# An attention and feed-forward kernel on one core: where V is made, when the Gram products run, and how the last two steps are ordered

## Chip, cores and metric

One core of a Trainium2 chip. The metric is the device time of one execution in microseconds. The kernel before took 211.31 us, the median of three runs (209.78 to 213.27).

## What is computed

x has 8 sequences of 1024 rows of 128 channels, float32. Two layers follow each other, each with a residual and a layer norm.

```python
def _L0_attn_ref(...):                       # 16 heads of 8 channels
    def proj_heads(W, bb):
        z = x + x @ W.T + bb                 # and split into heads
    q, k1, k2, v1, v2 = ...                  # five of these
    S1 = einsum('bhnd,bhne->bhde', k1, v1) / n
    S2 = einsum('bhnd,bhne->bhde', k2, v2) / n
    v1m, v2m = v1.mean(over rows), v2.mean(over rows)
    S12 = S1 * S2
    out = q@S1*v2m*g1 + S12.sum(axis=2)*g2 + q@S2*v1m*g3 + q@S12*g4
    return layernorm(out) * ln_g + ln_b  @ Wo.T + bo
def _L0_ffn_ref(...):                        # only expert 0 counts
    x = tgt + relu(tgt @ w1[0] + b1[0]) @ w2[0] + b2[0]
    return layernorm(x) * gamma + beta
x = layernorm(x + attn(x)); x = layernorm(x + ffn(x))
```

Attention has no softmax, so for each sequence it is a 128x128 matrix. It follows from the Gram matrix G = xᵀx (with the column sums of x beside it). S1 and S2 are heads of (I+Wk) G (I+Wv)ᵀ with terms for the biases.

## The kernel before

The rows are tiled in 16 groups of 512 (4 tiles of 128), two groups to a sequence (a "batch" in the code). A program of steps n = -2 to 15 runs on each engine (`run_steps`, `body`). In step n TensorE does, in this order: the products of x with the sequence's matrix for group n+1 (`product`, 16 matmuls into `z_ps`), `up` of group n (four chunks of the feed-forward's first weights), the transposes of x of group n+2 (`turn_x`), `down` of group n (16 matmuls of 128x128), and the transposes of x1 of group n+1 (`turn_x1`). ScalarE squares, takes roots, does the relus and writes the results; VectorE adds, takes statistics (`stats`), normalizes, and splits x, x1 and the matrices in a high and a low part for fp32r; POOL (GpSimd) adds and multiplies rows out of SBUF. Each engine's list is in a fixed order written out by hand, and semaphores join them, so an instruction that waits holds all that stands behind it on its engine.

**Preparing a sequence.** `gram(b)` makes G of sequence b in 8 matmuls, `gram_out` copies it. `gram_av(b)` makes two products: G·A_v (256 columns, for E), and the column sums, broadcast to 128 weight columns, with A_v (256 columns: V, the same row on all partitions). VectorE turns them to E (L769) and V (L775) and signals both by one semaphore, EV_out. `ak_e(b)` on TensorE, which waits for it, makes A_k·E; `s_out` makes S1 and S2 of it and V; `prepare(b)` makes M (on POOL, from batch 1 on); `attention_matrix(b)` and `centered(b)` make the matrices P and Q; ScalarE and VectorE split them (`PQ_upper`, `PQ_rest`). Even steps n from 2 to 12 prepare sequence (n+2)/2. Sequences 0 to 4 have their Gram products in steps -2 and -1; those of 5, 6 and 7 stand at the ends of steps 7, 9 and 11, around `turn_x1`.

**The start (step -2).** bv1 and bv2 are spread from HBM to 128 partitions, 64 KB each, on ScalarE's queue, behind the small vectors. The "late" vectors (ln_g, ln_b, b1) go on POOL's queue behind Wo and Wq; `turn_late` on TensorE waits for them and stands ahead of `ak_e(0)`. SP's queue carries x of sequence 0, Wk1, Wk2 and x of the others. `output_rows` needs the late vectors and Wo.

**The end (steps 14, 15 and what follows).** The last group's `down` goes in two halves to two PSUM banks. Behind step 15 VectorE runs `half_y2`, `half_y2n`, `half_y3`, `half_st4` and `half_res`: residual, statistics, normalizing, gamma, beta, again statistics and normalizing, half by half; POOL does y3 of half 0. ScalarE takes the roots between (`half_std`) and writes the results of group 14 (`result`, L580). The y2g and y3 of group 14 are on VectorE (L824, L827).

Of the kernel before, what the change touches and what calls it, by code (L numbers as in the profile page):

```python
# [42 lines left out]
EARLY = 5  # L43


def build(nc, x, Wq, bq, Wk1, bk1, Wk2, bk2, Wv1, bv1, Wv2, bv2, g1, g2, g3, g4, ln_g, ln_b, Wo, bo,
# [11 lines left out]
    with ctx:  # L58
# [24 lines left out]
        g_row = sb("g_row", [1, 4, HEADS])  # L83
        scale_row = sb("scale_row", [1, 128])
# [21 lines left out]
        V_sb = sb("V_sb", [128, 2, 128])  # L106
        S_sb = sb("S_sb", [128, 2, 128])
# [57 lines left out]
        bv_loaded = sem("bv_loaded")  # L165
# [51 lines left out]
        EV_out = sem("EV_out")  # L217
# [24 lines left out]
        end_y2n = sem("end_y2n")  # L242
        end_y2g = [sem("end_y2g0"), sem("end_y2g1")]
        end_y3 = [sem("end_y30"), sem("end_y31")]
# [3 lines left out]
        end_res = sem("end_res")  # L248
# [58 lines left out]

        def rows(t, n=TILES):
            return t.unsqueeze(1).to_broadcast([128, n, 128])
# [4 lines left out]
        def half_y3(eng, h):  # L314

            two_tiles, own = slice(2 * h, 2 * h + 2), (GROUPS - 1) % 2
            eng.wait_ge(end_y2n, h + 1)
            eng.tensor_tensor(y2g[:, two_tiles, :], y2n[:, two_tiles, :], rows(gamma_rows[:, :], 2), ALU.mult).then_inc(end_y2g[h], 1)
            eng.wait_ge(end_y2g[h], 1)
            eng.wait_ge(x1beta_out, GROUPS)  # L320
            eng.tensor_tensor(y3[own][:, two_tiles, :], y2g[:, two_tiles, :], x1beta[own][:, two_tiles, :], ALU.add).then_inc(end_y3[h], 1)

        def s_out(dve, b):

            wait(dve, EV_out, b + 1)
            wait(dve, s_done, b + 1)
            for j in range(2):
                last = dve.scalar_tensor_tensor(out=S_sb[:, j, :], in0=V_sb[:, 1 - j, :],
                                                scalar=cols[:, j:j + 1],
                                                in1=prep_ps[:, j * 128:(j + 1) * 128],  # L330
                                                op0=ALU.mult, op1=ALU.add)
            last.then_inc(S_out, 1)

        def prepare(eng, b):

            eng.wait_ge(EV_out, b + 1)
# [3 lines left out]
            eng.tensor_tensor(gv[:, :, :], V_sb[:, :, :], gmask[:, 0:2, :], ALU.mult).then_inc(m_step, 1)  # L340
# [18 lines left out]
        class Step:  # L359
            def __init__(self, n):  # L360
# [12 lines left out]
                self.gram = n % 2 == 1 and has(3) and self.seq(3) >= EARLY  # L373
# [12 lines left out]
        VECTORS = 16 * (4 + 3)  # L386
# [7 lines left out]
        def _(sp):  # L394
# [6 lines left out]
            for i, w in enumerate((Wk1, Wk2)):  # L401
                sp.dma_start(w_raw[:, 2 + i, :], w[:, :]).then_inc(kv_loaded, 16)
            for b in range(1, BATCHES):
                load_x(b)

            def store(b):
                for g in range(1 if b == BATCHES - 1 else SEQ_GROUPS):
                    wait(sp, res_out, b * SEQ_GROUPS + (g + 1))
# [4 lines left out]
            for h in range(2):  # L413
                t = TILES + 2 * h
                sp.wait_ge(end_res, h + 1)
# [7 lines left out]
        def _(pool):  # L423
# [25 lines left out]
            for i, v in enumerate((ln_g, ln_b)):  # L449
                pool.dma_start(late_rows[i:i + 1, :], row(v)).then_inc(late_loaded, 16)  # L450
            pool.dma_start(late_rows[2:6, :], b1[0, :].rearrange("(k c) -> k c", c=128)).then_inc(late_loaded, 16)
# [21 lines left out]
            def body(st):  # L473
# [6 lines left out]
                if st.prev and not st.last:  # L480
# [7 lines left out]
                if st.prev2 and not st.prep:  # L488
                    result_bias(n - 2)
# [24 lines left out]
            half_y3(pool, 0)  # L514
# [3 lines left out]
        def _(act):  # L518
            for i, w in enumerate((Wv1, Wv2)):
                act.dma_start(w_raw[:, i, :], w[:, :]).then_inc(kv_loaded, 16)  # L520
            for i, v in enumerate((bk1, bk2, bq)):
                act.dma_start(vec_rows[i:i + 1, :], row(v)).then_inc(vec_loaded, 16)
            for i, g in enumerate((g1, g3, g4, g2)):
                act.dma_start(g_row[:, i, :], row(g)).then_inc(vec_loaded, 16)
            for i, v in enumerate((bv1, bv2)):
                act.dma_start(bv_rows[:, i, :], spread(v)).then_inc(bv_loaded, 16)
# [5 lines left out]
            def less_bv():  # L532
                act.wait_ge(bv_loaded, 16 * 2)
                act.activation(nbv_rows[:, 0, :], bv_rows[:, 1, :], ACT.Copy, scale=float(SEQ))
                act.activation(nbv_rows[:, 1, :], bv_rows[:, 0, :], ACT.Copy, scale=float(SEQ)).then_inc(nbv_ready, 1)
# [16 lines left out]
            def squares(m):  # L552
# [8 lines left out]
                std(z_sum[:, :], std1, std1_out, 1.0 / C)  # L561

# [36 lines left out]
            def body(st):  # L599
# [7 lines left out]
                if st.prev:  # L607

                    wait(act, st3_out, n)
                    std(two(st3, 2), std3, std3_out, 1.0 / C)  # L610
                if st.nxt:
                    squares(n + 1)
                if st.cur:
# [4 lines left out]
                    relu(st, 2)  # L618
                    relu(st, 3)
# [11 lines left out]
                if st.prev2:  # L631

                    wait(act, st4_out, n - 1)
                    std(two(st4, 2), std4, std4_out, 1.0 / C)
# [6 lines left out]
                if st.nxt:  # L641
# [8 lines left out]
                if st.gram:  # L650
                    gram_out(st.seq(3))
# [10 lines left out]
            act.wait_ge(st4_out, GROUPS - 1)  # L662
            std(two(st4, 2), std4, std4_out, 1.0 / C)
            half_std(st3, std3, 1, end_st3, end_std3)
# [467 lines left out]
```

## Time and profile before

| | |
|---|---|
| median of 3 runs | 211.31 us |
| profiled execution | 209.8 us, its span 208.1 us |
| granted TensorE clock, mean | 0.989 of 2.4 GHz |
| TensorE busy | 191.7 us (92%), 1377 instructions |
| VectorE busy | 161.8 us (78%), 478 |
| GpSimd (POOL) busy | 136.3 us (66%), 177 |
| ScalarE busy | 127.8 us (61%), 383 |
| chain that ended last | PE 73%, DVE 12%, issue 4%, DMA 4%, POOL 4%, ACT 2% |

The profile is one execution. PE is TensorE's matmuls (L904 is a helper through which all of them go, so they are told apart by their tiles), PEld its weight loads, DVE is VectorE, ACT ScalarE, SP the engine that issues most DMAs. A product of float32 operands is two records of the profile, one of fp32r operands is one. Busy shares are means over stages that have different limits; what holds a stage is read from the chain of waits and from the waits themselves.

### The profile page before, as it was taken

How to read it: one execution, taken by the hardware profiler on the slowest of the kernel's cores; microseconds unless marked ns; L12 is line 12 of the kernel's file. 1: busy time of each engine (PE TensorE's matmuls, PEld its weight loads, DVE VectorE, ACT ScalarE, POOL GpSimd, SP SyncE). 2: the span in 40 equal slices, each digit the busy share in tenths (PEclk: the TensorE clock that was granted, in tenths of full speed). 3: DMA queues.
4: the chain of work that ended last, by engine and by line, in shares of the span. 5: the costliest groups of instructions: out<-in, count | busy, mean ns of one | idle time of the engine just before them, and what ended most of it. 6: DMA issues, size and time to landing. Idle time of an engine off the chain costs nothing.

```text
span 208.1 us, 4250 instructions
## 1 busy us (share of the span) xinstructions
PE 191.7 (92%) x1377; PEld 176.2 (85%) x1377; DVE 161.8 (78%) x478; ACT 127.8 (61%) x383; POOL 136.3 (66%) x177
## 2 busy tenths in 40 slices
PE   6949999999999999999999999999999999999930
PEld 6838998998898979897989999998989899988620
DVE  0265854988879887989698787977798869896895
ACT  0342439364659575966596667758585659785571
POOL 8904651474697758984898379756897389876130
PEclk9999999999999999999999999999999999999995
DMA  5999700000000100110010101010011001011012
GB/s 154 243 191 289 185 0 5 2 0 5 0 15 35 54 2 0 55 50 0 0 54 4 48 3 50 2 54 0 2 50 55 0 3 50 0 52 54 2 50 101
DMA packets 12116, 9.98 MB, mean 48 GB/s; under 512 B 727, under 2 KB 9950, under 8 KB 12094
## 3 DMA queue, kind: packets, MB, share of 16 engines
q1 hardware_dynamic: 11056, 8.52, 13.2%
q0 software_dynamic: 448, 0.92, 2.5%
q10 hardware_dynamic: 590, 0.26, 0.6%
q8 instruction: 11, 0.18, 0.3%
q14 instruction: 11, 0.09, 0.1%
HBM read 5.51 MB, written 4.19 MB: 47 GB/s over the span
## 4 chain that ended last, share of the span: by engine, by line
PE 73%; DVE 12%; issue 4%; DMA 4%; POOL 4%; ACT 2%; DVEq 0%; POOLq 0%; ACTq 0%
PE down_ps L904 25%; PE up_ps L904 20%; PE prep_ps L904 11%; PE z_ps L904 10%; DMA late_rows<-in_L_ffn_b 4%; PE turn_ps L1031 3%; PE turn_ps L1002 2%; DVE y2n L705 2%; DVE st L700 2%; DVE down_ps L749 2%; DVE E_sb L769 1%; DVE x1T_lo L840 1%; DVE y2n L870 1%; DVE V_sb L775 1%; ACT res L580 1%
## 5 line engine op out<-in xcount | busy, mean ns | idle before, releaser
L904 PE MATMUL down_ps<-w_sb,hT 128*128 128x128 f32 x496 | 61.0, 277 | 0.1
L904 PEld LDWEIGHTS down_ps<-w_sb,hT 128*128 128x128 f32 x496 | 58.4, 192 | 1.2 <-DVE y2n L705 0.4
L597 ACT ACTIVATE hT<-up_ps,cols 128x512 f32<-128x512 f32 x64 | 41.7, 681 | 4.4 <-PE up_ps L904 4.2
L580 ACT ACTIVATE res<-y,nb,rstd 128x128 f32<-128x128 f32 x60 | 24.7, 483 | 7.5 <-POOL nb L471 7.5
L509 POOL TENSOR_TENSOR x1b<-x,b_rows 128x512 f32<-128x512 f32 x16 | 20.6, 1286 | 10.1 <-DVE x L705 10.1
L904 PE MATMUL up_ps<-x1T_hi,w_hi 128*128 128x512 f32 x64 | 26.0, 406 | 0.5 <-ACT hT L597 0.5
L904 PE MATMUL up_ps<-x1T_lo,w_hi 128*128 128x512 f32 x64 | 25.4, 398 | 0.0
L904 PE MATMUL up_ps<-x1T_hi,w_lo 128*128 128x512 f32 x64 | 25.3, 396 | 0.0
L558 ACT ACTIVATE z_sq<-z_ps 128x128 f32<-128x128 f32 x64 | 16.8, 270 | 11.4 <-PE z_ps L904 11.4
L498 POOL TENSOR_TENSOR xu<-X,u_rows 128x512 f32<-128x512 f32 x16 | 19.0, 1187 | 6.0 <-DVE u_rows L696 6.0
L705 DVE TENSOR_SCALAR x<-z_ps,st,rstd 128x128 f32<-128x128 f32 x64 | 21.9, 404 | 0.1
L483 POOL TENSOR_TENSOR y2g<-y2n,gamma_rows 128x512 f32<-128x512 f32 x14 | 18.0, 1284 | 5.8 <-DVE y2n L705 5.8
L705 DVE TENSOR_SCALAR y2n<-down_ps,st,rstd 128x128 f32<-128x128 f32 x60 | 20.5, 405 | 0.5
L511 POOL TENSOR_TENSOR x1beta<-x,beta_rows 128x512 f32<-128x512 f32 x16 | 20.6, 1291 | 0.0
L904 PE MATMUL z_ps<-PQ_hi,xT_hi 128*128 128x256 f32 x64 | 20.5, 321 | 0.0
L799 DVE SCALAR_TENSOR_TENSOR z_ps<-z_ps,rstd,xu 128x128 f32<-128x128 f32 x64 | 18.2, 353 | 0.6
L487 POOL TENSOR_TENSOR y<-y2g,x1beta 128x512 f32<-128x512 f32 x14 | 17.8, 1273 | 1.1
L550 ACT ACTIVATE std<-st,eps_col 128x4 f32<-128x4 f32 x46 | 12.3, 295 | 9.6 <-DVE st L700 9.6
L904 PE MATMUL z_ps<-PQ_hi,xT_lo 128*128 128x256 f32 x64 | 18.0, 281 | 0.0
L904 PE MATMUL z_ps<-PQ_lo,xT_hi 128*128 128x256 f32 x64 | 17.9, 280 | 0.0
L904 PE MATMUL z_ps<-PQ_hi,spread 128*128 128x256 f32 x64 | 17.9, 279 | 0.0
L340 POOL TENSOR_TENSOR gv<-V_sb,gmask 128x256 f32<-128x256 f32 x7 | 5.2, 746 | 17.2 <-DVE V_sb L775 17.2
(151 smaller groups left out, 416.5 us busy)
## 6 DMA issues: line engine op xcount, KB each, us to landing
X<-in_L_attn_x SPq DMA_DIRECT2D x8, 512.0 KB, 9.9
out<-res SPq DMA_DIRECT2D x15, 256.0 KB, 2.0
w_sb<-in_L_ffn_w POOLq DMA_DIRECT2D x2, 256.0 KB, 9.8
out<-res SPq DMA_DIRECT2D x2, 128.0 KB, 1.9
w_raw<-in_L_attn_Wv ACTq DMA_DIRECT2D x2, 64.0 KB, 2.8
w_raw<-in_L_attn_Wk SPq DMA_DIRECT2D x2, 64.0 KB, 4.0
bv_rows<-in_L_attn_bv ACTq DMA_DIRECT2D x2, 64.0 KB, 6.0
g_row<-in_L_attn_g ACTq DMA_DIRECT2D x4, 0.1 KB
```

The source lines that it names most:

```text
L483: pool.tensor_tensor(y2g[:, :, :], y2n[:, :, :], rows(gamma_rows[:, :]), ALU.mult).then_inc(y2g_out, 1)
L487: pool.tensor_tensor(y3[(s - 1) % 2][:, :, :], y2g[:, :, :], x1beta[(s - 1) % 2][:, :, :], ALU.add).then_inc(y3_out, 1)
L498: pool.tensor_tensor(xu[s % 2][:, :, :], X[:, b, g * TILES:(g + 1) * TILES, 0:C], rows(u_rows[:, :]), ALU.add).then_inc(xu_out, 1)
L509: pool.tensor_tensor(x1b2[(s + 1) % 2][:, :, :], x1[:, :, :], rows(b2_rows[:, :]), ALU.add).then_inc(x1b2_out, 1)
L511: pool.tensor_tensor(x1beta[(s + 1) % 2][:, :, :], x1[:, :, :], rows(beta_rows[:, :]), ALU.add).then_inc(x1beta_out, 1)
L550: act.activation(dst[:, :], src, ACT.Sqrt, bias=eps_col[:, :], scale=scale).then_inc(done, 1)
L558: act.activation(z_sq[:, t, :], z_ps[t // 2][:, t % 2 * 256:t % 2 * 256 + C], ACT.Square, accum_out=z_sum[:, t:t + 1]).then_inc(sq_out, 1)
L580: last = act.activation(res[buf][:, t, :], y3[buf][:, t, :], ACT.Identity, scale=rstd4[:, t:t + 1], bias=nb4[:, t:t + 1])
L597: act.activation(hT[:, k, :], up_ps[k % len(up_ps)][:, :], ACT.Relu, bias=cols[:, 5 + k:6 + k]).then_inc(relu_out, 1)
L705: last = dve.tensor_scalar(dst[:, t, :], of_tile(t), st[:, t // 2, 3 * (t % 2) + 1:3 * (t % 2) + 2], rstd[:, t:t + 1], ALU.subtract, ALU.mult)
L799: last = dve.scalar_tensor_tensor(out=y1_tile(t), in0=y1_tile(t), scalar=rstd1[:, t:t + 1], in1=xu[(s + 1) % 2][:, t, :], op0=ALU.mult, op ...
L904: return pe.matmul(o, lhsT, rhs, start=start, stop=stop)
```

## The change

1. For sequences 2 to 7 `gram_av` makes only G·A_v. Their V comes from two products (`v_rows`): the column sums of three sequences are the three weight columns, and the result is three rows of 256. VectorE adds bv (`v_rest`), and SP spreads each row to 128 partitions by a DMA (`place_v`). E and V have a semaphore each.
2. The Gram products of sequences 5, 6, 7 stand in steps 1, 3, 5.
3. bv is loaded as one row and spread by a product with ones; ScalarE copies and scales it. The late vectors are on SP's queue, ahead of x(1).
4. E, V and A_k·E of sequence 1 are made in step -2, ahead of P of sequence 0; its S behind `PQ_rest(0)`. `ak_e(1)` writes a bank of its own.
5. In step 14 VectorE takes the statistics of y3(12) behind those of y1(15), and those of y3(13) and its root in the same step; in step 15 ScalarE takes the root of y2(14) behind three relus. y2g and y3 of group 14 are on POOL.
6. The last group: y2d = (y2 − mean)·gamma and y3 = y2d·rstd + x1beta, each a fused instruction, half by half on VectorE. The result of half 0 is on ScalarE. The second half of `down` goes to z_ps[0], the first to prep_ps.

```diff
+VSET = 3
-        last_ps = [down_ps[:, 0:2 * C], prep_ps[:, 0:2 * C]]
+        last_ps = [prep_ps[:, 0:2 * C], z_ps[0][:, 0:2 * C]]
+        bv_ps = up_ps[0][:, 0:256]
+        def s_bank(b):
+            return up_ps[1] if b == 1 else prep_ps
+        def v_of(b):
+            return V_sb[:, :, :] if b < 2 else V_all[:, b - 2, :, :]
...
-                self.gram = n % 2 == 1 and has(3) and self.seq(3) >= EARLY
+                self.gram = EARLY + n // 2 if n in (1, 3, 5) else None
+                self.v_set = {0: 0, 7: 1}.get(n)
+                self.v_rest = {1: 0, 7: 1}.get(n)
...   SP
+            for i, v in enumerate((ln_g, ln_b)):
+                sp.dma_start(late_rows[i:i + 1, :], row(v)).then_inc(late_loaded, 16)
+            sp.dma_start(late_rows[2:6, :], b1[0, :].rearrange("(k c) -> k c", c=128)).then_inc(late_loaded, 16)
             for b in range(1, BATCHES):
                 load_x(b)
+            def place_v(v):
+                sp.wait_ge(rows_out, v + 1)
+                for i in range(VSET):
+                    sp.dma_start(V_all[:, v * VSET + i, :, :]..., V_rows[i:i + 1, v, :, :]...to_broadcast([1, 128, 256])).then_inc(V_landed[v], 16)
             def store(b):
                 for g in range(1 if b == BATCHES - 1 else SEQ_GROUPS):
+                    if (b, g) in ((0, 0), (2, 1)):
+                        place_v(b // 2)
...   POOL
+                if st.last:
+                    result_bias(n - 2)
-                if st.prev and not st.last:
+                if st.prev:
...   ScalarE
+            for i, v in enumerate((bv1, bv2)):
+                act.dma_start(bv_row[:, i, :], row(v)).then_inc(vec_loaded, 16)
             for i, g in enumerate((g1, g3, g4, g2)):
                 act.dma_start(g_row[:, i, :], row(g)).then_inc(vec_loaded, 16)
-            for i, v in enumerate((bv1, bv2)):
-                act.dma_start(bv_rows[:, i, :], spread(v)).then_inc(bv_loaded, 16)
             def less_bv():
-                act.wait_ge(bv_loaded, 16 * 2)
+                act.wait_ge(bv_done, 1)
+                act.activation(bv_rows[...], bv_ps, ACT.Copy).then_inc(bv_ready, 1)
...
+                    if st.last:
+                        root3(n)          # between relu 2 and relu 3
+                if st.nxt and not st.nxt2:
+                    root4(n - 1)          # behind x1T_hi
             half_std(st3, std3, 0, end_st3, end_std3)
-            act.wait_ge(st4_out, GROUPS - 1)
-            std(two(st4, 2), std4, std4_out, 1.0 / C)
             half_std(st3, std3, 1, end_st3, end_std3)
+            root4(GROUPS - 2)
+            half_std(st_end, std_end, 0, end_st4, end_std4)
             result(GROUPS - 2, GROUPS % 2, BATCHES - 1)
-            half_std(st4, std4, 0, end_st4, end_std4)
-            half_std(st4, std4, 1, end_st4, end_std4)
+            half_std(st_end, std_end, 1, end_st4, end_std4)
+            act.wait_ge(end_nb, 1)
+            for t in range(2):
+                last = act.activation(res[own][:, t, :], y3[own][:, t, :], ACT.Identity, scale=rstd_end[...], bias=nb_end[...])
...   VectorE, step -2
                     prepare(dve, 0)
                     u_row()
+                    e_and_v(1)
                     xT_rest(0)
                     PQ_rest(0)
+                    s_out(dve, 1)
...   VectorE, step 14
                     stats(y1_pairs, st2, st2_out)
+                if st.nxt and not st.nxt2:
+                    y3_stats(n - 2, s % 2)
...
                     normalize(x1, y1_tile, st2, rstd2, x1_out)
-                if st.last:
-                    ...                   # y2g and y3 of group 14
+                if st.nxt and not st.nxt2:
+                    y3_stats(n - 1, 1 - s % 2)
...
+                if st.nxt and not st.nxt2:
+                    result_factors(n - 1)
...   VectorE, the end
+            half_y2(0); half_y2d(0); half_y3(0)
+            half_y2(1); half_y2d(1)
+            y3_stats(GROUPS - 2, 1 - own)
+            half_st4(0)
+            half_y3(1)
+            result_factors(GROUPS - 2); result_bias_here(GROUPS - 2)
+            half_st4(1)
+            half_r4(0)
+            dve.scalar_tensor_tensor(out=nb_end[:, half[0]], ...).then_inc(end_nb, 1)
+            half_r4(1)
+            ...                           # res of half 1, two tensor_scalar
...   TensorE
                 pe.transpose(vec_ps[:, 0:3], vec_rows[:, :], ident[0:3, 0:3])
+                mm(bv_ps, ones[0:1, :], bv_row[...]).then_inc(bv_done, 1)
             def gram_av(b):
+                if b >= 2:
+                    wait(pe, G_out, min(BATCHES, b + 4))
+                    mm(prep_ps[:, 0:256], G_sb[:, b, 0:C], A_kv[:, 0:2, :]...).then_inc(ev_done, 1)
+                    return
+            def v_rows(v):
+                b = 2 + v * VSET
+                pe.wait_ge(G_out, b + VSET)
+                pe.wait_ge(PQfix_out, 2 if v == 0 else 5)
+                mm(prep_ps[0:VSET, 0:256], G_sb[:, b:b + VSET, C], A_kv[:, 1:3, :]...).then_inc(rows_done, 1)
...   TensorE, step -2
                     turn_late()
+                    keep_warm(2)
                     ak_e(0)
                     output_rows()
                     gram(1, range(SEQ_TILES))
+                    gram_av(1)
                     attention_matrix(0)
                     centered(0)
+                    ak_e(1)
...   TensorE, step -1
-                    gram_av(1)
+                    pe.wait_ge(nbv_ready, 1)
                     gram(2, range(0, 3))
-                    product(0, 0, lambda: ak_e(1))
+                    product(0, 0)
...   TensorE, steps 0 to 15
                     up(n, 0)
                 if st.prep:
                     ak_e(st.prepared())
+                if st.v_set == 1:
+                    v_rows(1)
...
+                if st.v_set == 0:
+                    v_rows(0)             # last of step 0
```

## Rows read from the trace of the kernel before

**Rows 1.** Stages: window, its length, busy us of each engine, granted clock, DMA

```profile
10.00:20.00 10.00, 6.70 (x49) 6.02 (x48) 5.25 (x17) 3.25 (x10) 2.83 (x3) 1.00 1.00 230
...
39.19:60.92 21.73, 21.22 (x154) 19.43 (x154) 18.14 (x54) 13.15 (x41) 14.88 (x18) 1.00 0.00 1
...
104.40:127.17 22.77, 22.77 (x171) 21.32 (x170) 18.97 (x57) 15.67 (x49) 16.64 (x21) 1.00 0.07 25
...
199.30:208.10 8.80, 0.00 (x0) 0.00 (x0) 6.07 (x20) 3.13 (x10) 1.72 (x2) 0.73 0.25 89
```

**Rows 2.** Waits of TensorE over the whole run: us, times, longest

```profile
PE z_ps L930 <- DMA late_rows<-in_L_ffn_b: 2.2, 1, 2.2
...
PE prep_ps L904 <- DVE V_sb L775: 1.5, 3, 0.5
```

**Rows 3.** The chain of waits in order of time: start, us, what

```profile
5.30 7.52 DMA late_rows<-in_L_ffn_b
...
15.03 1.79 PE up_ps L904 x16
16.82 0.35 PE prep_ps L904 x4
...
25.75 0.46 POOL M_sb L351
...
30.06 1.88 PE z_ps L904 x16
...
51.88 0.34 DVE V_sb L775
...
116.28 0.86 PE prep_ps L904 x4
...
118.79 0.44 PE prep_ps L904 x4
```

**Rows 4.** Timeline of the start: start us, us, engine, line, operation

```profile
1.59 4.26 PE L904 MATMUL down_ps<-ident 128*128 128x128 f32 x20 [1.59 <-POOL ident L428]
...
9.00 1.10 PE L904 MATMUL prep_ps<-A_kv,G_sb 128*128 128x256 f32 x4
...
11.93 0.48 DVE L769 SCALAR_TENSOR_TENSOR E_sb<-bv_rows,G_sb,prep_ps 128x256 f32<-128x256 f32 x1 [2.63 <-DMA bv_rows<-in_L_attn_bv]
...
14.35 0.46 PE L904 MATMUL z_ps<-WoT,lnb_wide 128*128 128x128 f32 x2 [0.63 <-ACT Wog L544]
```

**Rows 5.** DMAs: issuer, count, KB each, median us from issue to landing

```profile
out<-res SPq DMA_DIRECT2D x15, 256.0 KB, 2.0
...
w_raw<-in_L_attn_Wk SPq DMA_DIRECT2D x2, 64.0 KB, 4.0
bv_rows<-in_L_attn_bv ACTq DMA_DIRECT2D x2, 64.0 KB, 6.0
```

**Rows 6.** Timeline of VectorE in step 8, which a Gram product precedes

```profile
117.76 0.42 DVE L775 TENSOR_TENSOR V_sb<-prep_ps,nbv_rows 128x256 f32<-128x256 f32 x1
```

**Rows 7.** Timeline of the last two steps and the end

```profile
188.84 0.20 POOL L471 TENSOR_TENSOR nb<-mr,minus 128x4 f32<-128x4 f32 x1
...
193.37 0.30 ACT L550 ACTIVATE std<-st,eps_col 128x4 f32<-128x4 f32 x1 [2.16 <-DVE st L700]
193.57 2.47 ACT L597 ACTIVATE hT<-up_ps,cols 128x512 f32<-128x512 f32 x4
...
197.11 0.69 DVE L827 TENSOR_TENSOR y<-y2g,x1beta 128x512 f32<-128x512 f32 x1
...
197.21 0.65 POOL L471 TENSOR_TENSOR nb<-mr,minus 128x4 f32<-128x4 f32 x1
...
200.51 1.65 ACT L580 ACTIVATE res<-y,nb,rstd 128x128 f32<-128x128 f32 x4
...
205.01 1.04 SPq L416 DMA_DIRECT2D out<-res  x2
205.09 0.60 DVE L870 TENSOR_SCALAR res<-y,st,rstd 128x128 f32<-128x128 f32 x2
```

More of the change, by code:

```diff
@@ L384, in run_steps @@
                 body(Step(n))
[L386 removed]
+        VECTORS = 16 * (4 + 3 + 2)
         LATE_VECTORS = 16 * 3
@@ L487, in body @@
                     pool.tensor_tensor(y3[(s - 1) % 2][:, :, :], y2g[:, :, :], x1beta[(s - 1) % 2][:, :, :], ALU.add).then_inc(y3_out, 1)
-                if st.prev2 and not st.prep:
+                if st.prev2 and not st.prep and not st.last:
                     result_bias(n - 2)
@@ L561, in squares, with root3, root4 @@
                 std(z_sum[:, :], std1, std1_out, 1.0 / C)
+            def root3(n):
+                wait(act, st3_out, n)
+                std(two(st3, 2), std3, std3_out, 1.0 / C)
+            def root4(m):
+                wait(act, st4_out, m + 1)
+                wait(act, r4_out, m)
+                std(two(st4, 2), std4, std4_out, 1.0 / C)
             def PT_copy(b):
@@ L606, in body @@
                     gram_out(1)
-                if st.prev:
-                    wait(act, st3_out, n)
-                    std(two(st3, 2), std3, std3_out, 1.0 / C)
+                if st.prev and not st.last:
+                    root3(n)
                 if st.nxt:
@@ L618, in body @@
                     relu(st, 2)
+                    if st.last:
+                        root3(n)
                     relu(st, 3)
@@ L630, in body @@
                     std(two(st2, 2), std2, std2_out, 1.0 / C)
-                if st.prev2:
-                    wait(act, st4_out, n - 1)
-                    std(two(st4, 2), std4, std4_out, 1.0 / C)
+                if st.prev2 and not st.last:
+                    root4(n - 2)
                 if st.prep:
@@ L811, in body @@
                     dve.reciprocal(rstd2[:, :], std2[:, :]).then_inc(r2_out, 1)
-                if st.prev2:
+                if st.prev2 and not st.last:
                     result_factors(n - 2)
@@ L860, in half_y2, with half_y2d, half_y3 @@
                 dve.bn_stats(st3[:, h, :], last_ps[h].rearrange("p (t c) -> p c t", c=C)).then_inc(end_st3, 1)
-            def half_y2n(h):
+            def half_y2d(h):
+                wait(dve, sq_out, GROUPS * TILES)
+                dve.wait_ge(end_st3, h + 1)
+                for t in range(2 * h, 2 * h + 2):
+                    last = dve.scalar_tensor_tensor(out=y2d[:, t, :], in0=y2_last(h, t % 2),
+                                                    scalar=st3[:, h, 3 * (t % 2) + 1:3 * (t % 2) + 2], in1=gamma_rows[:, :],
+                                                    op0=ALU.subtract, op1=ALU.mult)
+                last.then_inc(end_y2d, 1)
+            def half_y3(h):
                 dve.wait_ge(end_std3, h + 1)
@@ L901, in _ @@
+            last.then_inc(end_res[1], 1)
         @block.tensor
@@ L1080, in body @@
                 if st.cur:
-                    wait(pe, y2n_out, n)
+                    if not st.last:
+                        wait(pe, y2n_out, n)
                     for t in range(TILES):
```

176 lines of the change are left out of this document (99 added, 77 removed).

## The prediction

> **What bounds the kernel now.** I read the stages first, cut at the starts of the products that open a step [rows 1]. From 30 to 181 us TensorE is busy nearly all the time, at a granted clock of 1.00 (2.4 GHz). Before 20 us it is not (6.70 of 10 us busy), and in the last 8.80 us it has nothing to do. So a saving on TensorE counts in the middle, and a saving on a chain of the other engines counts at both ends. A pair of steps (an odd one and the even one behind it, which prepares a sequence) takes 21.73 us in the first three pairs and 22.77 us in the last three; only the latter hold a Gram product, and there TensorE is never idle. The waits of TensorE [rows 2] show why: 2.2 us once for the late vectors, and in the middle only three waits of 0.5 us for V. The chain of waits [rows 3] runs at the start through the late vectors' DMA (7.52 us) and in the first pairs through VectorE: `down` ends, y2 is added, its statistics and y2n follow, then E and V, then `ak_e` on TensorE. In the last pairs it stays on TensorE. The end is a chain of VectorE and ScalarE [rows 7].
>
> **The sum is made against the profiled execution**: span 208.1 us, 209.8 us in all. That was the fastest of the kernel's runs; the median is 211.31 us, 1.5 above it. I take the same difference off the median.
>
> **Step 1, the start (to the product of group 1, 30.06 us).** The late vectors now follow x(0) and Wk on SP's queue, three issues of about 0.4 us ahead of x(1); from their neighbour on that queue (Wk, 4.0 us to landing, [rows 5]) I have them by 7 to 8 us. x(1) starts 1.1 us later; it is first read near 15 [rows 3], which hides that. POOL issues three DMAs less, so the rows and w1, w2 come 1.5 us earlier. E of batch 0 started at 11.93 after 2.63 us of idle for the 64 KB spread of bv [rows 4]. Now bv is a product of one contracted row and 256 columns: priced like half of the G·A pair (0.86 us in the chain for two products, [rows 3]), 0.43 us. It delays `gram_av(0)` from 9.00 [rows 4] to about 9.4, which ends at 10.3. ScalarE's copy and two scalings of bv (estimated at 1 us together) run beside it. E then starts at 10.4: 1.5 us earlier. The rows u and zw, which waited for Wog until 14.35 [rows 4], go at 12.6, and `gram(1)` ends near 15.1 instead of 16.8.
>
> There the new order takes something back. `gram_av(1)` comes ahead of P of batch 0: TensorE waits for the copy of the Gram matrix (0.28 us and two hand-overs, 0.45) and does 0.86 us of products, so `attention_matrix(0)` goes at 16.2 instead of 16.82: 0.65 gained. Behind it `ak_e(1)` (0.44) fills the wait for PQ. The product of group 0 then starts 0.7 earlier, and it no longer has `ak_e(1)` and its wait in its middle: turn_x(1) comes 1.4 earlier than now. M of batch 1 ended at 26.2 on POOL [rows 3]; its S is now ready some 2.5 us earlier, ahead of the second half of the product, and so it is off the path. What is late next is x1 of group 0 on VectorE, which follows the product: 1.4 earlier. TensorE finds it at 27.0, does `turn_x1(0)` and the second half of `gram(4)`, and opens step 0 at 28.3 instead of 30.06 [rows 3]. **Gain 1.7 us.** The bounds: if the two more vectors on ACT's queue land late (the last g is issued 0.55 later, and its landing shows nowhere), TensorE waits ahead of everything and 0.9 is left, at the worst 0; if the whole wait of 2.2 us goes, it is 2.2. I take 1.7, since no wait for a g is named today [rows 2].
>
> **Step 2, six batches with V from two products.** Each `gram_av` of batches 2 to 7 drops one of two products: 0.43 us of TensorE's time. The two products `v_rows` have 3 columns of weights but 256 moving columns. No row shows a product with three columns of weights; the bounds are 0.1 us (the four records of `attention_matrix`, two of 130 columns and two of one, take 0.35 together, [rows 3], so a small product can be nearly free) and 0.43; I take 0.43, by the like moving width. VectorE drops V (0.42 us busy, 0.34 in the chain [rows 3]) six times and has two additions on three partitions instead (at most 0.42 each); those stand in steps 1 and 7 behind y2n, where [rows 2] shows no wait of TensorE, so nothing.
>
> **Step 3, the Gram products of batches 5 to 7 move from steps 7, 9, 11 to 1, 3, 5.** The first three pairs become what the last three are, less the dropped product: 22.77 − 0.43 = 22.34, that is +0.61 each, +1.83. TensorE has no wait there: V was ready at 118.18 [rows 6] and TensorE came at 118.79 [rows 3]; 0.43 earlier it still finds E ready. The last three pairs become what the first three are: bound by VectorE, with E alone to wait for: 21.74 − 0.34 = 21.40, that is −1.37 each, −4.11. The dropped product gives nothing there; it only lengthens TensorE's wait to about 0.6. To it add `v_rows(1)` in step 7 and `v_rows(0)` at the end of step 0, 2 × 0.43. **Net 1.83 − 4.11 + 0.86 = −1.42 us.** Without the wait effect it is bounded by pure TensorE work, 6 × 0.43 − 0.86 = 1.7 less; with cheap `v_rows` it is 2.1.
>
> The spread of V to 128 partitions is six DMAs of 128 KB on SP's queue, ahead of the stores. A store of 256 KB landed in 2.0 us, a 64 KB spread at full load in 6.0 [rows 5]: 2 to 8 us for three. The first set is issued near 41 us and read near 50; the second a step and a half ahead. The stores behind them wait on buffers used again two steps later. Cost nothing; without that cover 1 us a set. Behind it on its engine gv of POOL and S of VectorE would wait, and through M the next P; with V there they don't.
>
> **Step 4, the last two steps.** Statistics of y3(12) leave the path ahead of y1(15) (0.77), but rstd4(12) still precedes x1(15), and now waits for ScalarE behind these: x1(15) comes 0.15 earlier. In the last step root3 no longer holds the four relus (ScalarE idled 2.16 us for it [rows 7]); the relus end at 195.2 instead of 196.04, so the first half of `down` ends at 196.6 instead of 197.48. From there VectorE works through: y2, statistics, y2d and y3 of half 0 to 199.0; the same of half 1 to y2d, 200.5; statistics of y3(14) 0.76, of half 0 0.38, y3 of half 1 0.77, factors 0.35: nb of group 14 at 202.75. It was 200.47. Then ScalarE: result(14), 1.65 us [rows 7], stands ahead of the square root of half 1; that ends at 204.7, and both halves' results at 205.4 and 205.5. VectorE ended at 205.69 [rows 7]; but the two stores are now issued back to back, half a microsecond (1.04 for two, [rows 7]) late. **Net 0.1 us slower**; bounds 0.9 faster (if half 1's root slips ahead) and 0.7 slower. The y2g and y3 of group 14 on POOL (196.2 to 198.9) are ready before VectorE asks for y3 at 200.5.
>
> A thing speaks against this placing. While VectorE ran y3 with two inputs from SBUF, POOL's tiny nb took 0.65 us instead of 0.20 [rows 7]. In the new order y3 of half 0 (two SBUF inputs) falls on POOL's y3(14). If it has to stand still there until POOL's ends at 198.9, that is 0.4 us; I keep 0.1 for the step and have 0.4 within its upper bound of 0.7. The Trainium skill (SBUF — State Buffer, "Who interferes with whom") says that a VectorE instruction with two SBUF inputs and a GpSimd instruction that reads SBUF exclude each other, whichever comes second waiting for the whole of the first. By that rule, with which the trace agrees in kind, the sum would end 0.4 higher.
>
> **Sum.** −1.7 − 1.4 + 0.1 = −3.0 us: span 205.1, execution 206.8, on the median **208.3 us**.
>
> **Rivals.**
> A. *The start gives nothing.* The vectors on ACT's queue land near 9.5 to 10, or another transfer comes last. For: bv's landing of 6.0 us on this queue [rows 5]. Against: no wait for a g now [rows 2]. Gain 1.3 to 2: 209.3 to 210 us.
> B. *More at both ends.* The start gives its 2.2, `v_rows` cost 0.1 each, the end 0.9 from the earlier relus: −2.2 − 2.1 − 0.9 = −5.2, 206.1 us. For: the relus' end is sure; against: result(14) stands in ScalarE's order.
> C. *Slower than before: TensorE starves at the start and loses its clock.* It runs in order, and `turn_vectors` now needs nine small DMAs. If the last lands like bv's spread did, whose reader started at 11.93 [rows 4], TensorE idles some 3.4 us and everything comes 1.1 us later than now instead of 1.7 earlier. The granted clock fell to 0.73 on average over the last 8.80 us, after TensorE stopped [rows 1]; today's 2.2 us gap left it at 1.00. What a fall costs is seen at the launch: 20 records of 128 columns took 4.26 us, 0.213 each [rows 4], the pace of 1.2 GHz, where such records are 0.112 apart later (16 in 1.79 us, [rows 3]). As long a stretch here would lose 2.1 us: +1.1 + 2.1 − 1.4 + 0.1 = +1.9, 213.2 us. It decides from a landing of about 11.5 us on; with the clock kept it is −0.2.
> D. *The moved Gram products only move the waits*: another wait of VectorE's chain (x1 for `turn_x1`) holds the late pairs at more than 21.4, and the terms of steps 2 and 3 together come to 0: −1.7 + 0.1, 209.7 us. For: late pairs lose their cover. Against: pairs of this kind ran at 21.73 with one wait only [rows 1, 2].
>
> **Chances.** Forecast 0.5 (range of its own 206.3 to 209.8, with the scatter of the runs, 209.78 to 213.27 for three of the same kernel), A 0.15, B 0.18, C 0.07, D 0.10. Of the whole, 8 in 10 lie in **205.2 to 211.2**. Two per cent is about what a measurement of this kernel can tell from no change; that is 207.1. The forecast lies 1.4% below the median, B 2.5%. Faster by over 2%: 0.3 of the forecast by scatter, 0.75 of B, little of the rest: 0.30. Slower by over 2%: a third of C and scatter on D and the rest, 0.05. Same: 0.65.
>
> **What would show it.** Right if: TensorE's waits no longer name the late vectors; E of batch 0 starts near 10.4; the product of group 1 starts at 28 to 28.7; pairs from there take 22.3, 22.3, 22.3, then 21.8, 21.4, 21.4, with waits of 0.5 to 0.6 for E in the last three only; in the last step the chain ends over nb(14), result(14) on ScalarE and the root of half 1. Wrong if TensorE waits for a DMA ahead of 9 us, if a wait for E stands in the first pairs, or if POOL's y3(14) ends after 200.

## The result: 6.9% slower, and the profile after

| | before | after |
|---|---|---|
| median | 211.25 us | 224.49 us (4 runs, 224.23 to 224.97) |
| ratio after/before, 95% interval | | 1.069 [1.064, 1.075] |
| profiled execution, span | 209.8, 208.1 us | 224.23, 222.5 us |
| granted TensorE clock, mean | 0.989 | 0.952 |

The forecast was 208.3, the range up to 211.2: wrong in sign and by 16 us. I cut both traces where the product that opens a step starts; the places add up to the whole difference of the spans.

```
stretch                    before   after   after-before  forecast
launch to product of gr.1   29.81   29.64      -0.17        -1.7
step 0 (v_rows(0))           9.13    9.83      +0.70        +0.43
pair 1 (steps 1, 2)         21.74   29.29      +7.55        +0.61
pair 2                      21.74   22.34      +0.60        +0.61
pair 3                      21.74   22.33      +0.59        +0.61
pair 4 (7, 8; v_rows(1))    22.77   30.31      +7.54        -0.94
pair 5                      22.77   21.42      -1.35        -1.37
pair 6                      22.76   21.40      -1.36        -1.37
step 13                      9.14    9.13      -0.01         0
steps 14, 15 and the end    26.50   26.81      +0.31        +0.1
sum                                           +14.4         -3.0 (with rounding)
```

Four pairs of six came out within 0.02 us of the forecast. Two are 6.9 and 8.5 us longer than forecast, and these are the two in which a set of spread V is first read. Their even steps, beside a like step that nothing disturbs, in the windows of the kernel after (window, length, busy us of PE, PEld, DVE, ACT, POOL, granted clock, DMA share, GB/s); they answer to [rows 1]:

```profile
50.43:68.76 18.33, 14.20 (x85) 13.00 (x84) 8.98 (x28) 8.04 (x24) 9.51 (x14) 0.81 0.34 13
79.69:91.10 11.41, 11.41 (x85) 10.65 (x84) 8.90 (x27) 7.29 (x23) 7.00 (x12) 1.00 0.01 2
123.27:143.74 20.47, 14.58 (x85) 13.04 (x84) 10.09 (x31) 8.48 (x25) 11.67 (x15) 0.83 0.42 27
152.88:165.16 12.28, 11.68 (x85) 10.58 (x84) 10.02 (x30) 7.73 (x24) 8.82 (x13) 1.00 0.06 22
```

Steps 2 and 8 issue as many matmuls (85) as steps 6 and 12, but take 18.33 and 20.47 us where 11.41 and 12.28 would do: 6.92 + 8.19 = 15.1 us, more than the whole loss. TensorE's waits in the kernel after (us, times, longest), which answer to [rows 2], hold the first part of it:

```profile
PE prep_ps L974 <- POOL M_sb L368: 9.4, 2, 5.3
PE prep_ps L974 <- DVE E_sb L806: 1.8, 3, 0.6
...
PE z_ps L994 <- DMA g_row<-in_L_attn_g: 0.6, 1, 0.6
```

The late vectors' 2.2 us are gone, and the three waits of 0.6 for E stand in the last three pairs, as forecast. But 9.4 us stand in two waits for M. Who holds M up is seen in the timeline of step 2 (start, us, engine, line, operation; in brackets the idle time before it and what ended it):

```profile
42.31 0.40 DVE L830 TENSOR_TENSOR V_rows<-prep_ps,nbv_rows 3x256 f32<-3x256 f32 x1
...
42.74 3.46 SPq L432 DMA_DIRECT2D V_all<-V_rows  x3
...
58.85 0.61 DVE L344 SCALAR_TENSOR_TENSOR S_sb<-V_all,cols,prep_ps 128x128 f32<-128x128 f32 x2 [5.00 <-DMA V_all<-V_rows]
58.85 0.72 POOL L357 TENSOR_TENSOR gv<-V_all,gmask 128x256 f32<-128x256 f32 x1 [8.42 <-issue]
...
62.09 0.45 POOL L368 TENSOR_TENSOR M_sb<-M_half,S12g 128x128 f32<-128x128 f32 x1
...
62.59 0.80 PE L974 MATMUL prep_ps<-AqT,M_sb 128*128 128x130 f32 x2 [4.13 <-POOL M_sb L368]
```

V's rows are there at 42.7, the three DMAs are issued at once, and S and gv start together at 58.85, 16 us later: VectorE stood 5.00 us for them. (The 8.42 of POOL is put down to "issue", because the profile had no releaser for it; that it starts in the same hundredth as S suggests that it waited for the same thing.) The view of the tile V_all names the transfers' own times, from issue to landing:

```profile
L432 SPq DMA_DIRECT2D V_all<-V_rows x6: 481/602/2255, 42.7 to 118.6; - x6
...
DMA to landing us min/median/max: 6.9/11.2/15.0
```

The three of a set land 6.9, 11.2 and 15.0 us after issue. They share one semaphore, and `wait_v` asks for the whole set, so sequence 2, whose own V was there after 6.9, waits for sequence 4's.

The rest is TensorE's clock. Three stretches of step 2 and of what follows, around the wait, and the products of `down` ahead of the wait and behind it:

```profile
60.00:64.00 4.00, 1.41 (x6) 1.41 (x7) 3.56 (x12) 0.77 (x3) 3.69 (x7) 0.65 0.01 2
64.00:68.00 4.00, 4.00 (x17) 3.64 (x16) 0.85 (x2) 1.58 (x4) 3.92 (x5) 0.50 0.00 0
68.00:72.00 4.00, 4.00 (x31) 3.78 (x31) 3.33 (x9) 2.98 (x14) 1.14 (x1) 1.00 0.17 66
...
56.51 1.95 PE L974 MATMUL down_ps<-w_sb,hT 128*128 128x128 f32 x16
...
66.17 2.40 PE L974 MATMUL down_ps<-w_sb,hT 128*128 128x128 f32 x12
```

After the wait of 4.13 us TensorE is busy all the time and issues 17 records in 4 us, at a granted clock of 0.50 (1.2 GHz). A record of `down` takes 0.20 us there (12 in 2.40), ahead of the wait 0.12 (16 in 1.95). From 68 us on the clock is 1.00 again. So the engine is not only late here: what it does in the next 5.4 us takes nearly twice as long.

### The profile page after: what moved, and what is told of

Its sections match the earlier page's. It is cut to its first block and busy times, and to the rows that moved or that the text cites. A ratio compares the mean times of both kernels' runs of the same rounds, so it can differ in the third digit from the quotient of the medians.

```text
span 222.5 us, 4276 instructions
## 1 busy us (share of the span) xinstructions
PE 197.5 (89%) x1375; PEld 180.5 (81%) x1375; DVE 158.3 (71%) x473; ACT 130.2 (59%) x386; POOL 134.5 (60%) x174
## 5 line engine op out<-in xcount | busy, mean ns | idle before, releaser
L974 PE MATMUL down_ps<-w_sb,hT 128*128 128x128 f32 x480 | 61.8, 285 | 0.1
L974 PEld LDWEIGHTS down_ps<-w_sb,hT 128*128 128x128 f32 x480 | 59.5, 200 | 0.9 <-ACT hT L638 0.3
L638 ACT ACTIVATE hT<-up_ps,cols 128x512 f32<-128x512 f32 x64 | 42.5, 682 | 6.3 <-PE up_ps L974 6.1
L513 POOL TENSOR_TENSOR y2g<-y2n,gamma_rows 128x512 f32<-128x512 f32 x15 | 19.2, 1283 | 13.9 <-DVE y2n L752 13.9
L517 POOL TENSOR_TENSOR y<-y2g,x1beta 128x512 f32<-128x512 f32 x15 | 19.1, 1274 | 1.2
L686 ACT ACTIVATE x1T_hi<-turn_ps 128x512 fp32r<-128x512 f32 x16 | 9.5, 592 | 12.4 <-PE turn_ps L1092 12.2
## 6 DMA issues: line engine op xcount, KB each, us to landing
V_all<-V_rows SPq DMA_DIRECT2D x6, 128.0 KB, 11.2
```

The source lines that it names most:

```text
L513: pool.tensor_tensor(y2g[:, :, :], y2n[:, :, :], rows(gamma_rows[:, :]), ALU.mult).then_inc(y2g_out, 1)
L517: pool.tensor_tensor(y3[(s - 1) % 2][:, :, :], y2g[:, :, :], x1beta[(s - 1) % 2][:, :, :], ALU.add).then_inc(y3_out, 1)
L638: act.activation(hT[:, k, :], up_ps[k % len(up_ps)][:, :], ACT.Relu, bias=cols[:, 5 + k:6 + k]).then_inc(relu_out, 1)
L974: return pe.matmul(o, lhsT, rhs, start=start, stop=stop)
```

## The experiments

Each is the kernel after with one edit, except where said, and timed in turns with the kernel before on the same chip. The experiments ran on three chips. The kernel before has a median of 209.34 us beside e1 to e4, 209.52 beside e5, e6, e8 and e10, and 210.62 beside e11 and e12, where it had 211.25 beside the kernel after. So medians of different groups can't be compared to a microsecond; the ratios and the parts of the profiles are the better measure.

### e1: a semaphore for each spread

The theory: the one-partition source makes the spreads slow, and the shared semaphore makes the first reader pay for all three.

```diff
-        V_landed = [sem("V_landed0"), sem("V_landed1")]
+        V_landed = [sem(f"V_landed{i}") for i in range(2 * VSET)]
...
-                eng.wait_ge(V_landed[(b - 2) // VSET], 16 * VSET)
+                eng.wait_ge(V_landed[b - 2], 16)
...
-  V_rows[i:i + 1, v, :, :]....to_broadcast([1, 128, 256])).then_inc(V_landed[v], 16)
+  V_rows[i:i + 1, v, :, :]....to_broadcast([1, 128, 256])).then_inc(V_landed[v * VSET + i], 16)
```

> The changed kernel with one semaphore for each of the six spreads of V instead of one for each set of three; nothing else differs. Theory (the third spread of a set lands 16 us after the issue of the first, but the first alone lands within 7 us): S of sequence 2 and of sequence 5 finds its V, the waits of TensorE for M_sb (4.1 and 5.3 us) and the stretches at half clock behind them go; steps 2 and 8 take 11.4 and 12.3 us instead of 18.3 and 20.5: 224.5 - 15.1 = 209.4 us. Rival 1 (the three spreads share the DMA engines evenly and all land late together): no change, 224 us. Rival 2 (the wait is for POOL, whose gv stands at the head of its queue, not for the landing as such): the waits shrink by half, 216 to 218 us.

Measured: 208.70 us, ratio to before 0.994 [0.991, 0.998], span 206.8. The spreads are as slow as ever (6.9/11.2/15.1), but no wait for M is left. First step 2 of this kernel in the windows, then its V_all tile:

```profile
49.87:61.27 11.40, 11.40 (x85) 10.65 (x84) 8.91 (x27) 7.28 (x23) 6.78 (x12) 1.00 0.55 21
```

```profile
L432 SPq DMA_DIRECT2D V_all<-V_rows x6: 476/602/2279, 42.2 to 111.1; - x6
...
DMA to landing us min/median/max: 6.9/11.2/15.1
```

Step 2 takes 11.40 instead of 18.33 us although the spreads run beside it (DMA share 0.55). So the waits for the set account for the whole loss, and no other wait comes from the slow transfers. The six pairs are 22.36, 22.34, 22.34, 22.11, 21.41 and 21.42 us.

### e2: the same bytes from 128 partitions

Theory against rival: one partition read 128 times is slow, or every SBUF to SBUF spread of 128 KB is. This kernel leaves out the real V of sequences 2 to 7; only its time and its transfers are read.

```diff
-  V_rows[i:i + 1, v, :, :]....to_broadcast([1, 128, 256])).then_inc(V_landed[v], 16)
+  nbv_rows[:, :, :].rearrange("p j c -> p (j c)")).then_inc(V_landed[v], 16)
```

> The changed kernel, but the six DMAs to V_all read 128 partitions of a tile in SBUF (each partition its own row) instead of one partition 128 times; same bytes, same destination, same packets of 1 KB. V of sequences 2 to 7 is thus wrong data; the time is what is looked at. Theory (one source partition is what makes the spread slow, 128 KB in about 5 us each): the DMAs land in about 2 us each, no wait for M_sb is left, 209.4 us. Rival (any SBUF to SBUF DMA of 128 KB in 1 KB packets is that slow, or the destination is): landings of 7, 11 and 15 us as before, 224 us.

Measured: 208.36 us, from a single execution, with the shared semaphore kept, and no wait for M. Its V_all tile:

```profile
L432 SPq DMA_DIRECT2D V_all<-nbv_rows x6: 471/601/602, 42.0 to 110.9; - x6
...
DMA to landing us min/median/max: 1.9/2.1/2.1
```

The window from 42 to 62 us, in the view of the DMA queues (GB/s in 40 slices of 0.5 us; packets, MB, share of 16 engines), of the kernel after and then of this one:

```profile
GB/s 0 0 0 8 35 27 29 33 27 25 25 27 29 33 27 23 25 27 31 31 29 14 31 27 33 31 27 16 31 27 33 55 10 0 0 0 16 0 0 0
...
q1 hardware_dynamic: 432, 0.39, 57.5%
```

```profile
GB/s 0 0 209 164 166 248 0 0 0 0 0 0 0 49 0 0 0 0 0 0 0 0 0 0 0 0 0 0 0 0 0 0 0 0 0 0 0 0 0 0
...
q1 hardware_dynamic: 432, 0.39, 5.8%
```

The same 432 packets and 0.39 MB, a tenth of the engines' time. What is slow is the source: one partition gave some 27 GB/s to all the DMA engines together. That a few engines did the work is excluded by the share: 57.5% of 16 engines over 20 us is 11.5 us for all of them, of the 16 from the first issue to the last landing. The Trainium skill (DMA: Bandwidth & Descriptors, "Rules for kernel authors") has all 16 engines at work when the outermost dimension that is not 1 is a multiple of 16, here 128; with that the share agrees, but the rule does not bring the speed. Whether it matters that it is one partition, or that the same 1 KB is read again and again, e2 does not separate: it changes both. Either edit alone, e1's or e2's, takes the loss away, so it needs both the slow source and the shared semaphore.

### e4: work for TensorE in the wait

The wait stays, but 17 and 22 products that nobody reads fill it: what is gained is the clock's part.

```diff
+                        if t == 2 and st.prep and st.prepared() in (2, 5):
+                            pe.wait_ge(relu_out, n * FCH + FCH)
+                            keep_warm(17 if st.prepared() == 2 else 22)
                         if t == 2 and st.prep:
                             attention_matrix(st.prepared())
```

> The changed kernel with 17 and 22 products of 128 columns that nobody reads, on TensorE ahead of attention_matrix of sequences 2 and 5, where it waits 4.1 and 5.3 us for M_sb (they fill 3.8 and 4.9 us of it). Theory (of the 15.1 us, 9.4 are waits and 5.7 are TensorE at 1.2 GHz behind them): the clock stays at 2.4 GHz, 224.5 - 5.7 = 218.8 us. Rival (the 5.7 us are other waits, on ScalarE and VectorE behind M): 224 to 225 us.

Measured: 218.37 us, ratio 1.041 [1.036, 1.047], span 216.7, mean clock 0.987. Steps 2 and 8 in the windows:

```profile
49.68:65.61 15.93, 15.46 (x119) 14.52 (x118) 8.81 (x27) 7.39 (x23) 7.00 (x12) 1.00 0.40 15
120.16:138.00 17.84, 16.86 (x129) 15.57 (x128) 9.90 (x30) 7.84 (x24) 9.05 (x13) 1.00 0.48 32
```

At full clock they take 15.93 and 17.84 us, against 18.33 and 20.47: 5.0 us of the 15.1 were the clock (2.4 and 2.6), the other 10 the wait itself (e4 lies 9.9 us of span above e1). The theory had 5.7.

### e3: V of every sequence from its own product again

All other parts of the change stay. It prices "V from two products" once the spreads are in time.

```diff
...
                     mm(prep_ps[:, 0:256], G_sb[:, b, 0:C], A_kv[:, 0:2, :]...)
+                    mm(prep_ps[:, 256:512], G_sb[:, b, C:C + 1].to_broadcast([128, 128]), A_kv[:, 1:3, :]...)
...
-                self.v_set = {0: 0, 7: 1}.get(n)
+                self.v_set = None
```

> The changed kernel with V of every sequence again from a second product in gram_av and its addition on VectorE (no v_rows, no spread by DMA); start, order of the Gram products and last two steps stay changed. Theory (all of the loss is the late V, two v_rows cost 0.70 each, and apart from that V from two products gives 3 x 0.43 + 3 x 0.34): no late V, 224.5 - 15.1 - 1.4 + 2.3 = 210.3 us, that is 0.9 slower than with a V that lands in time and 1 faster than the kernel before. Rival (the moved Gram products or the start lose by themselves): 213 us or more.

Measured: 209.49 us, ratio 0.999 [0.996, 1.002]. Its pairs take 22.78, 22.76, 22.78 and then 21.80 three times; those of e1 are 0.42, 0.42 and 0.44 shorter at first, and 0.39 later where no `v_rows` is in them. The forecast had 0.43 and 0.34 a sequence. Its profile also had a worse start (the product of group 1 at 30.42, with a wait of 1.1 us for a g vector, and from 12 to 15 us a granted clock of 0.51, shown further below), which the medians need not share: they differ by 0.8 us.

### e10: the kernel before with only the Gram products moved

> The kernel before with one change: the Gram products of sequences 5, 6 and 7 stand in steps 1, 3 and 5 instead of 7, 9 and 11. Theory (a pair of steps with a Gram product takes 22.77 us and one without 21.73, wherever it stands): no change, ratio 1.000 to the kernel before. Rival (the early steps have cover to spare that the late ones lack, or the other way round): the times of the pairs differ from 22.77 and 21.73 by more than 0.1 us each.

Measured: 210.36 us, ratio 1.003 [0.999, 1.007]. Pairs 22.75, 22.77, 22.77, then 21.74, 21.73, 21.72: the move exchanges the two kinds of pair and gains nothing alone. By the prices of the pairs it would gain nothing with the smaller V either (three at 22.34 and three at 21.40, in either order), though no run shows that by itself; what it does is to have the column sums of sequences 5 to 7 ready for `v_rows(1)` in step 7. Rival D is out: no other wait holds the late pairs, here or in the kernel after (21.42 and 21.40).

### e5 and e6: the start (both on e1)

e5 takes the four g vectors out of the first wait: they get a semaphore, and their product stands behind `gram_av(0)`.

> The kernel of e1_sem_each, and the four small g vectors have a semaphore of their own; their product stands behind gram_av(0), and VectorE copies its result behind E and V of sequence 0. Theory (at the start TensorE waits in order for the last g, 0.3 to 0.6 us, and does 0.3 us for it ahead of gram_av(0), though E needs only bv): E of sequence 0 starts 0.6 to 0.9 us earlier and the product of group 1 likewise: 208.0 us. Rival (another chain of the start ends last, by way of Wo and the late vectors): no change, 208.7 us.

Measured: 208.51 us, ratio 0.994 [0.991, 0.998]: no gain. `gram_av(0)` starts at 9.78 as in e1 (9.79), and the way from there to the product of group 0 takes 10.36 instead of 9.93.

e6 takes back part 4 of the change: `gram_av(1)` behind P of sequence 0, `ak_e(1)` in the middle of the first product.

> The kernel of e1_sem_each with sequence 1 prepared where it was before: gram_av(1) behind P of sequence 0 and ak_e(1) in the middle of the first product. bv by a product and the late vectors on the queue of x stay. Theory (bringing gram_av(1) ahead of P puts 0.4 us of waiting and 0.9 us of products on the path to the first product, and what it saves behind, 0.44 and a wait of 0.13, is less): the first product starts 1.3 us earlier and the product of group 1 0.7 us earlier, 208.0 us. Rival (the preparation ahead is what gains at the start): M of sequence 1 is late again and the product of group 1 starts at 29.1 or later, 208.7 to 209.5 us.

Measured: 208.41 us, ratio 0.994 [0.989, 0.998]. In its profile the g vectors came late (a wait of 1.7 us), so I measure from `gram_av(0)`: to the product of group 1 it is 18.71 us, against 19.29 in e1 and in the kernel after. It reaches group 0's product 1.02 earlier and takes 0.44 longer behind it. So, by these profiles, preparing sequence 1 ahead of P costs 0.6 us; it doesn't gain. The ratio is that of e1, so the medians alone don't show it.

### e8: another order of the end (on e1)

In the part shown ScalarE takes half 1's root ahead of the result of group 14; both halves' results are on VectorE and their stores go out first.

```diff
             half_std(st_end, std_end, 0, end_st4, end_std4)
+            half_std(st_end, std_end, 1, end_st4, end_std4)
             result(GROUPS - 2, GROUPS % 2, BATCHES - 1)
-            half_std(st_end, std_end, 1, end_st4, end_std4)
...
```

> The kernel of e1_sem_each; at the end ScalarE takes the root of half 1 ahead of the results of group 14, VectorE writes the results of both halves of group 15, and SP stores these ahead of those of group 14. Theory (the end waits for ScalarE: result(14), 1.65 us, stands ahead of the root of half 1, VectorE idles 1.3 us for it): the last store is issued 0.7 us earlier, 208.0 us. Rival (VectorE's own work or the stores end last anyway): 208.5 to 208.8 us.

Measured: 208.25 us, ratio 0.993 [0.989, 0.997]. From the last product to the end 25.95 us, against 26.77 in e1 and 26.50 before. The kernel after's timeline shows what was removed; it answers to [rows 7]:

```profile
211.72 1.27 POOL L517 TENSOR_TENSOR y<-y2g,x1beta 128x512 f32<-128x512 f32 x1
...
212.45 0.95 DVE L935 SCALAR_TENSOR_TENSOR y<-z_sq,rstd,x1beta 128x128 f32<-128x128 f32 x2
213.06 0.34 DVE y L935
...
216.01 0.62 DVE L935 SCALAR_TENSOR_TENSOR y<-z_sq,rstd,x1beta 128x128 f32<-128x128 f32 x2
...
216.95 1.65 ACT L621 ACTIVATE res<-y,nb,rstd 128x128 f32<-128x128 f32 x4 [0.70 <-DVE nb L788]
218.50 0.28 ACT L698 ACTIVATE std<-st,eps_col 128x2 f32<-128x2 f32 x1
218.81 0.17 DVE L946 RECIPROCAL rstd<-std 128x2 f32<-128x2 f32 x1 [1.30 <-ACT std L698]
```

The root stands behind `result` of group 14 (1.65 us), and VectorE idles 1.30 for it. (The line without an operation is from the chain of waits: start, us, what.)

### e11 and e12: the parts together

e11 is e1 with the edits of e6 and e8, e12 the same with e5's as well.

> e1_sem_each with the start order of e6_old_start_order and the end of e8_end_order. Theory (the two gains are independent: from gram_av(0) to the product of group 1 it is 18.71 us in e6 against 19.29 in e1; from the last product to the end 25.95 against 26.77): 0.6 + 0.8 less than e1, 207.3 to 207.6 us, if the g vectors land no later than in e1. Rival (the start is set by when the g vectors land, which differs from run to run by more than that): 208 us and above.

> e11_sem_start_end with the g vectors' product behind gram_av(0), as in e5_g_behind. Theory (late g vectors then hold E of sequence 0 no more, which takes the scatter of up to 1.7 us of waiting away, though the mask made from them comes later): the median as e11 or up to 0.4 lower, and the runs closer together. Rival (the g vectors stay on the path by way of the mask that POOL makes of them): 0.3 to 0.5 slower than e11.

Measured: 207.41 us, ratio 0.988 [0.983, 0.992], and 207.38 us, ratio 0.987 [0.983, 0.992]; spans 205.7 and 205.5. e11 is within the 207.3 to 207.6 expected, and its profile has both gains again: 18.71 us from `gram_av(0)` to the product of group 1, 25.92 from the last product to the end. Both kernels beat the kernel before by 1.3% and, by the two ratios, the change by 7.6%. The 1.3% is against the median; against the faster of the two groups in which the runs of the kernel before lie (208.64 to 209.51 us beside e11; more on them below) it is 1.0% or less. e5's edit adds nothing that can be told, and the runs did not come closer together (206.84 to 207.91 in e12, 207.22 to 208.01 in e11).

## Why the prediction was wrong

**The step that failed** is the spread of V: "2 to 8 us for three [...] Cost nothing; without that cover 1 us a set." The last of three landed 15.0 us after its issue, and the two sets cost 15.1 us in all. I priced a DMA by its bytes, between a store from 128 partitions and a spread from HBM [rows 5], and neither row has the one thing that decides here, a single SBUF partition as the source of all. e2 shows that this is the cause of the slow landing, e1 that the shared semaphore turns it into a loss. Two more slips are in the same sentence. The 6.0 us in [rows 5] are for one DMA, and I took 8 as the end for three, where three behind one another at the slow row's pace would be near 18. And "without that cover" was priced without TensorE's clock, though rival C held that very mechanism. Its place was wrong (the start), not its size: with a wait of 4.13 us the granted clock fell to 0.50, and e4 puts 2.4 and 2.6 us on the two falls, where rival C had 2.1 for one. The right question was in the text ("gv of POOL and S of VectorE would wait, and through M the next P"), with the answer "they don't". And no rival and none of the signs of being wrong looked at the spread, so nothing in the prediction would have pointed at it.

**Start, forecast 1.7, measured 0.17** (0.73 in e1, whose g vectors were in time). The product of group 1 was to start at 28.1 (29.81 − 1.7) and started at 29.64. Of these 1.5 us, 0.95 lie ahead of `gram_av(0)`, which started at 10.35 and not at 9.4, so that E of sequence 0 started at 11.52 and not at 10.4:

```profile
1.59 4.64 PE L974 MATMUL up_ps<-ident 128*128 128x128 f32 x20 [1.59 <-POOL ident L459]
6.36 1.25 PE L974 MATMUL prep_ps<-X 128*128 128x130 f32 x8
...
9.49 0.22 PE L994 MATMUL z_ps<-ident,vec_rows 3*128 3x3 f32 x1 [0.56 <-DMA g_row<-in_L_attn_g]
9.58 0.67 PE L974 MATMUL up_ps<-bv_row,ones 1*128 1x256 f32 x2
...
10.35 1.13 PE L974 MATMUL prep_ps<-A_kv,G_sb 128*128 128x256 f32 x4
11.52 0.48 DVE L806 SCALAR_TENSOR_TENSOR E_sb<-bv_rows,G_sb,prep_ps 128x256 f32<-128x256 f32 x1 [0.77 <-PE prep_ps L974]
```

The wait for a g vector is 0.56, the case behind the low bound that I named. The rest was there before it: the 20 records of the launch took 4.64 us instead of 4.26 [rows 4], so the Gram products of sequence 0 began at 6.36, without a wait for x(0); in the kernel before they began at 6.07, behind a wait of 0.22 for x(0). The other 0.6 us lie behind `gram_av(0)`: that is the order of sequence 1, which I had as a gain, and e6 shows as a loss. Rival A (the start gives nothing) held there: the vectors came last, and even with them in time (e1) the start gave less than half of the 1.7.

**Step 2, the products.** The dropped product and V gave nearly what was forecast (e3 against e1). `v_rows` costs 0.70 us and not 0.43. The timeline has it at the end of step 0, and in step 2 a product with as many moving columns and 128 columns of weights:

```profile
38.94 0.60 PE L974 MATMUL prep_ps<-A_kv,G_sb 128*3 128x256 f32 x2
39.47 0.19 PEld L974 LDWEIGHTS z_ps<-PQ_hi,xT_hi 128*128 128x128 f32 x1 [0.43 <-issue]
...
51.45 0.60 PE L974 MATMUL prep_ps<-A_kv,G_sb 128*128 128x256 f32 x2
51.67 0.19 PEld L974 LDWEIGHTS z_ps<-PQ_hi,xT_hi 128*128 128x128 f32 x1
```

Three columns of weights save nothing over 128 (0.60 us both), and the next weights start 0.53 us after it and not 0.22: 0.27 us more in the step, twice. Why they start later is not shown. **Step 3, the moved Gram products**: right in both kinds of pair, and null alone (e10).

**Step 4, the end**: forecast +0.1, measured +0.31. The order was right (root of half 1 behind `result`), and so was the doubt about y3 of half 0: it took 0.95 us beside POOL's y3 and 0.62 alone, in the lines shown above. By the rule of the Trainium skill (SBUF — State Buffer, "Who interferes with whom"), VectorE's second instruction would stand until POOL's ends at 212.99; in the chain of waits its last part starts at 213.06, so the trace agrees.

**The sum without the failed step.** e1 has a span of 206.8 and a median of 208.7, where I said 205.1 and 208.3: −0.7 at the start, +0.7 for `v_rows(0)`, −1.5 in the pairs and +0.3 at the end. That the median of e1 lies so near the forecast is luck: the forecast was 1.4% below the kernel before, and e1 is 0.6% below the runs beside it [0.991, 0.998]. So even with V in time the change gives less than half of what was forecast.

**What stays open.** Why the first product follows `gram_av(0)` later when sequence 1 is prepared ahead was measured, not taken apart. The start itself varies from execution to execution: in e10's profile the wait for the late vectors was 1.4 us, and the granted clock fell right behind it; in e3's (last line) it fell too, behind a wait of 1.06.

```profile
11.89 0.22 PE L930 MATMUL z_ps<-ident,late_rows 6*128 6x6 f32 x1 [1.40 <-DMA late_rows<-in_L_ffn_b]
...
12.00:15.00 3.00, 2.45 (x10) 2.09 (x11) 2.29 (x10) 1.46 (x5) 0.00 (x0) 0.63 0.99 163
...
12.00:15.00 3.00, 3.00 (x15) 2.98 (x15) 1.59 (x8) 1.15 (x5) 0.00 (x0) 0.51 0.87 267
```

The profile in front had a longer wait there (2.2 us) and kept 1.00 [rows 1, 2]. The kernel before's times lie in two groups some 2 us apart (on e5's chip 16 of 31 runs at 208.4 to 209.5, the others from 210.3), while e1's mostly stay together (nine of ten at 208.1 to 208.9). The mean granted clock of the first group is 0.984 to 0.992, that of the second 0.984 or less and mostly 0.981 to 0.983; e10's profiled run, with the fall, has 0.981. That the two groups are the clock at the start is therefore likely, but not shown.

## What to carry to other kernels

Price a DMA by what it reads from, not by its bytes alone: a row in one partition, spread to 128, landed in 6.9 us for 128 KB, and the two queued behind it in 11.2 and 15.0. Give each transfer that has its own reader its own semaphore; here that one edit was worth 15 us. And where a new wait can fall on TensorE, add the clock to it: 5.0 us on 9.4 us of waits in this kernel, half as much again.

## What the runs showed of the hardware

- One SBUF partition as source of a spread gave about 27 GB/s in all, with 57.5% of 16 DMA engines' time over 20 us taken by it: three DMAs of 128 KB, issued within 1.2 us, landed 6.9, 11.2 and 15.0 us after their issues; from 128 partitions it is 1.9 to 2.1 us (e2).
- A float32 product with 3 weight columns and 256 moving columns occupies TensorE as long as one with 128 weight columns (0.60 us of records), but costs the step 0.70 us and not 0.43, as the next weights start later behind it.
- Granted clock after waits of TensorE: 0.50 behind 4.13 us, but at the start 0.63 behind one of 1.40 (e10), 0.51 behind one of 1.06 (e3) and 1.00 behind one of 2.2 (the kernel before). The length of the wait alone does not tell whether it falls.
- A VectorE instruction with two SBUF inputs took 0.95 us beside a GpSimd instruction from SBUF and 0.62 alone; its last part started 0.07 us after the other's end.
